# Equal-token attention scores as elementwise products on GpSimd, summed by sixteen small matmuls

## The reference, cut to what matters

```python
q, k, v, a = (c[..., 0], c[..., 1], c[..., 2], c[..., 3])       # complex, per head and channel
mag2 = a.real * a.real + a.imag * a.imag
a = a * (jax.lax.rsqrt(mag2) * jax.nn.sigmoid(jnp.log(mag2)))
kv = jnp.einsum('blhd,blhe->blhde', k, v)
...
_, h = jax.lax.associative_scan(comb, (a_e, kv), axis=1)        # h_t = a_t * h_(t-1) + k_t v_t
y = jnp.einsum('blhd,blhde->blhe', q, h)
```

## Time and profile before

| | |
|---|---|
| device time, 3 runs | 3787.07 us median, 3783.72 to 3789.23 |
| the profiled execution | 3780.13 us, of which its span is 3778.3 us |
| mean granted TensorE clock | 0.828 |
| busy over the span | PE 2900.2 us (77%), DVE 2067.0 (55%), ACT 1153.3 (31%), POOL 652.2 (17%) |
| chain of work that ended last | PE 59%, DVE 19%, ACT 7%, POOL 5%, issue 4% |

### The profile page before, as it was taken

How to read it: one execution, slowest core, us unless ns; L and a number is a source line. 1 busy time by engine, 2 the same in 40 slices (tenths; PEclk the granted TensorE clock), 3 DMA queues, 4 the chain that set the end, 5 groups by cost and what they waited for, 6 DMA issues and landing times.

```text
span 3778.3 us, 81987 instructions
## 1 busy us (share of the span) xinstructions
PE 2900.2 (77%) x35840; PEld 2145.9 (57%) x35840; DVE 2067.0 (55%) x4544; ACT 1153.3 (31%) x2220; POOL 652.2 (17%) x682
## 2 busy tenths in 40 slices
PE   4358869877986898699769877987688549999990
PEld 3244557545744664575457545744554538888880
DVE  4445676576658666856686676658443830000104
ACT  0212353135314432533353135314412512222220
POOL 0322400520060016003400520051000000000006
PEclk8678878888788878798878887888889769999995
DMA  2122201210121122012201220121100016565545
GB/s 81 23 57 51 43 5 42 68 40 15 48 69 19 41 46 56 8 41 57 46 7 41 62 46 8 47 67 24 41 29 28 2 52 205 190 200 192 193 158 174
DMA packets 230022, 247.56 MB, mean 66 GB/s; under 512 B 147360, under 2 KB 187168, under 8 KB 227360
## 3 DMA queue, kind: packets, MB, share of 16 engines
q1 hardware_dynamic: 223520, 225.54, 20.8%
q0 software_dynamic: 6144, 16.79, 1.4%
HBM read 196.15 MB, written 46.14 MB: 64 GB/s over the span
## 4 chain that ended last, share of the span: by engine, by line
PE 59%; DVE 19%; ACT 7%; POOL 5%; issue 4%; DMA 1%; SPq 0%; POOLq 0%; DVEq 0%
PE banks L1816 13%; PE banks L2326 7%; PE banks L2345 7%; PE banks L2049 4%; POOL arena L1708 3%; PE banks L2118 3%; PE banks L2138 2%; PE banks L2143 2%; PE banks L1826 2%; POOL arena L1752 2%; PE banks L2073 2%; PE banks L1948 2%; PE banks L1943 2%; PE banks L1953 1%; PE banks L1922 1%
## 5 line engine op out<-in xcount | busy, mean ns | idle before, releaser
L1708 POOL TENSOR_TENSOR arena<-arena 128x1 f32<-128x1 f32 (+30 forms) x496 | 435.1, 908 | 605.3 <-DMA arena<-n_d 438.2
L1168 DVE TENSOR_REDUCE arena<-arena 128x1 f32<-128x1 f32 (+30 forms) x496 | 243.6, 502 | 173.2 <-POOL arena L1708 168.8
L1729 POOL DMA_INDIRECT h_d<-h_tok,pos_now x64 | 66.4, 1037 | 1570.5 <-DVE pos_now L1573 1553.4
L2118 PE MATMUL banks<-arena 32*32 32x64 f32 (+2 forms) x6144 | 203.2, 317 | 162.3 <-DVE arena L1473 97.1
L1816 PE MATMUL banks<-hT,ring 128*128 128x512 f32 x640 | 310.6, 638 | 9.6 <-DVE arena L1312 8.9
L2118 PE MATMUL banks<-arena,xn 32*32 32x64 f32 (+2 forms) x6144 | 185.5, 305 | 149.1 <-DVE xn L1473 122.1
L2118 PEld LDWEIGHTS banks<-arena 32*32 32x32 f32 (+2 forms) x6144 | 180.3, 191 | 201.7 <-DVE arena L1473 117.1
L2326 PE MATMUL banks<-arena 128*128 128x256 f32 x1248 | 276.8, 381 | 0.0
L2345 PE MATMUL banks<-arena 128*128 128x256 f32 x1248 | 275.7, 380 | 0.0
L1020 ACT ACTIVATE arena<-banks,arena 128x256 f32<-128x256 f32 x312 | 130.7, 470 | 456.1 <-PE banks L2326 456.1
L2118 PEld LDWEIGHTS banks<-arena,xn 32*32 32x32 f32 (+2 forms) x6144 | 171.5, 186 | 167.9 <-DVE xn L1473 135.1
(11 more groups left out here) (340 smaller groups left out, 5251.4 us busy)
## 6 DMA issues: line engine op xcount, KB each, us to landing
arena<-in_w_ring SPq DMA_DIRECT2D x78, 1024.0 KB, 5.1
ring<-in_w_ring SPq DMA_DIRECT2D x104, 512.0 KB, 4.9
arena<-h_d SPq DMA_DIRECT2D x39, 256.0 KB, 5.3
y_d<-arena SPq DMA_DIRECT2D x39, 256.0 KB, 5.8
n_d<-NA SPq DMA_DIRECT2D x8, 1024.0 KB, 3.8
arena<-n_d SPq DMA_DIRECT2D x16, 512.0 KB, 8.1
u_d<-arena SPq DMA_DIRECT2D x8, 1024.0 KB, 3.8
NA<-u_d SPq DMA_DIRECT2D x32, 256.0 KB, 5.8
```

Source lines behind the costliest of these rows:

```text
L1168: dve.tensor_reduce(Usub[:, c, 0:t, t], part, AX.X, ALU.add).then_inc(*up(sub_sum, me))
L1708: pool.tensor_tensor(part, Usub[:, c, 0:t, 0:t], Nsub[:, c, t, 0:t].unsqueeze(1).to_broadcast([P, t, t]), ALU.mult)\
L2118: i_ = mm(bank[4 * hg + h][keys, b * width:(b + 1) * width], K2[rows_, r, b, keys], q, start=(r == 0), stop=(r == 1), skip_group_check=True)
```

## The change

For each hg, GpSimd multiplies q with k of the same token, channel by channel: four products of 128 x 1024 in a segment, two for each hg, written to ring slots 4, 0 and 1 and to `hT`. The two for hg wait for plane 5 (or 11) out of PSUM, for -q, and for `plane_mm` 8 (or 12), the last reader of the slots. PE sums each over the channels of a head with sixteen matmuls of 128 x 128 weights (the products) by 4 columns (`head_of`, ones for a head's channels), where it had 128 matmuls of 32 x 32 weights by 64 columns. DVE spreads the sum with the same predicated copy, whose source is now the sum, broadcast along tokens. The copy now waits for `scored`; the sum into q waits for GpSimd's `same_ok` in its place. On ACT, hg 1's `mag_sqrt` moves ahead of planes 10 and 11, and `take_keys(0)` ahead of `fill_state(1)`. The fills of the ring slots now wait for `scored` of both.

```diff
@@ ScalarE
                                 act.activation(Q3[:, 0], Q3[:, 2], ACT.Copy, scale=-1.0).then_inc(*up(q_neg, me))
-                            if n == 3:
-                                mag_sqrt(0)
-                    mag_sqrt(1)
+                            if c == 3:
+                                mag_sqrt(hg)
...
                     take_outputs(0)
+                    take_keys(0)
                     fill_state(1)
-                    take_keys(0)
                     take_keys(1)
@@ VectorE
                         if k == 0:
+                            dve.wait_ge(*at(scored, hg + 1))
...
-                                banks_[:, 4 * hg:4 * hg + HP, 0:2 * B * BLK].rearrange("p h (g t) -> p h g t", g=2 * B))\
-                                .then_inc(*up(masked, me))
+                                bank[4 * hg][:, 0:HP * 2 * B].rearrange("p (g h) -> p h g", h=HP).unsqueeze(3)
+                                .to_broadcast([P, HP, 2 * B, BLK])).then_inc(*up(masked, me))
...
-                        dve.wait_ge(*at(scored, hg + 1))
+                        dve.wait_ge(*at(same_ok, 2 * (hg + 1)))
                         step(dve.tensor_tensor(q2, t1[:, :, :], t2[:, :, :], ALU.add))
@@ GpSimd
-                    pool.wait_ge(*at(plane_mm, 6 * HG))
+                    for hg in range(HG):
+                        pool.wait_ge(*at(plane_ok, 6 * hg + 6))
+                        pool.wait_ge(*at(q_neg, hg + 1))
+                        pool.wait_ge(*at(plane_mm, 8 + 4 * hg))
+                        for r in range(2):
+                            pool.tensor_tensor(same_token[hg][r].rearrange("p (c t) -> p c t", c=2),
+                                               Q3s[hg][:, 1 - r:3 - r].rearrange("p c b t -> p c (b t)"),
+                                               K2s[hg][:, r].rearrange("p b t -> p (b t)").unsqueeze(1).to_broadcast([P, 2, NT]),
+                                               ALU.mult).then_inc(*up(same_ok, me))
+                    pool.wait_ge(*at(scored, HG))
                     pool.wait_ge(*at(v_mm, B))
@@ TensorE
+                    def same_tokens(hg):
+
+                        pe.wait_ge(*at(same_ok, 2 * (hg + 1)))
+                        if hg:
+                            pe.wait_ge(*at(v3_ok, 1))
+                        for b in range(B):
+                            for c in range(2):
+                                at_ = (2 * b + c) * HP
+                                for r in range(2):
+                                    t = slice(c * NT + b * SEG, c * NT + (b + 1) * SEG)
+                                    i_ = mm(bank[4 * hg][:, at_:at_ + HP], same_token[hg][r][:, t], const("head_of"),
+                                            start=(r == 0), stop=(r == 1))
+                        i_.then_inc(*up(scored))
...
-                    for k in range(STEPS):
+                    pe.wait_ge(*at(plane_ok, 6 * HG))
+                    for b in range(B):
+                        value_columns(b)
+                        if b == 1:
+                            same_tokens(0)
+                    same_tokens(1)
+                    for k in range(1, STEPS):
                         for hg in range(HG):
                             level(hg, k)
```

More of the change, by code:

```diff
@@ L274, in build @@
                  for v in (h_tok[:, :, :].rearrange("p b d -> p (b d)"), y2_flat[:, 2 * NT:4 * NT])]
+        same_token = ((ring[:, 4, :], ring[:, 0, :]), (ring[:, 1, :], hT[:, :, :, :].rearrange("p k b t -> p (k b t)")))
         first_raws = [score[:, :, :, :, SEG - BLK + i * BLK // 2:SEG - BLK + (i + 1) * BLK // 2] for i in range(HG)]
@@ L436, in build @@
         rt_exp = signal("rt_exp", rest=1)
+        same_ok = signal("same_ok", rest=4)
         zeroed = signal("zeroed", rest=6)
@@ L1736, in turn @@
                     settle()
-                counted(seg, [zeroed, sub_mul])
+                counted(seg, [zeroed, sub_mul, same_ok])
                 pool.sem_inc(started.handle, 1)
@@ L2079, in level @@
                         lev = k - 1
-                        if k == 0:
-                            pe.wait_ge(*at(plane_ok, 6 * HG))
+                        if lev:
+                            pe.wait_ge(*at(k_ready, 2 * lev + hg - 1))
+                        if lev == 0:
+                            pe.wait_ge(*at(masked, hg + 1))
                             if hg:
                                 pe.wait_ge(*at(v3_ok, B))
-                        else:
-                            if lev:
-                                pe.wait_ge(*at(k_ready, 2 * lev + hg - 1))
-                            if lev == 0:
-                                pe.wait_ge(*at(masked, hg + 1))
-                            elif lev <= INNER:
-                                pe.wait_ge(*at(block_ok, 2 * (lev - 1) + hg + 1))
-                            else:
-                                pe.wait_ge(*at(laid_middle, hg + 1))
-                        pe.wait_ge(*(at(q_ready, 2 * (k - 1) + hg + 1) if k else at(q_neg, hg + 1)))
+                        elif lev <= INNER:
+                            pe.wait_ge(*at(block_ok, 2 * (lev - 1) + hg + 1))
+                        else:
+                            pe.wait_ge(*at(laid_middle, hg + 1))
+                        pe.wait_ge(*at(q_ready, 2 * lev + hg + 1))
                         for b in range(B):
                             for r in range(2):
-                                for x in range(HP * NCH if k == 0 else 2 * HP if lev == INNER else HP):
+                                for x in range(2 * HP if lev == INNER else HP):
                                     h = x % HP
@@ L2099, in level @@
                                     q = Q3[rows_, 1 - r:3 - r, b]
-                                    if k == 0:
-                                        n = (h + x // HP) % NCH
-                                        keys = slice(BLK * n, BLK * n + BLK)
-                                        q = q[:, :, keys]
-                                        width = 2 * BLK
-                                    elif lev < INNER:
+                                    if lev < INNER:
                                         keys = slice(0, SEG)
@@ L2119, in level @@
                                             start=(r == 0), stop=(r == 1), skip_group_check=True)
-                            if k == 0 and hg == 0:
-                                if b == B - 1:
-                                    i_.then_inc(*up(scored))
-                                value_columns(b)
-                        if k or hg:
-                            i_.then_inc(*up(scored))
+                        i_.then_inc(*up(scored))
                     def outputs(hg):
```

## The result

| | before | after |
|---|---|---|
| median of 7 runs, us | 3783.72 (3771.18 to 3789.23) | 3821.38 (3805.88 to 3829.67) |
| ratio to before, 95% interval | | 1.0096 [1.0083, 1.0109] |
| profiled execution, us | 3780.1 | 3818.91 |
| its span, us | 3778.3 | 3817.1 |
| mean granted clock | 0.828 | 0.808 |

The changed kernel is slower by 1.0%, some 36 us by the ratio and 37.7 us between the medians. It issues 7,104 instructions fewer (74,883 for 81,987), and takes longer.

The account below looks back on a forecast made before the run. No engine bounds the mixer stage; the chain passes between PE, ACT and DVE. Eight segments' +35 us and the keys' -20 gave +15 on 3780.1, so 3795, and 3802 with the runs' 7 us median difference; range 3755 to 3845.

Parts of the forecast that it names:

- step 3: PE's start in the mixer stage, behind plane 11: from 439.2 to 441.3, late by 2.1 us.
- step 4: PE's work until `scored` of hg 1, all at the high clock level: 460.6 against 462.1, a gain of 1.5 us.
- step 5: PE's clock in the mixer stage: falls three times, 3.9 us each, 11.8 us at half speed, costing 5.9 us more.
- step 6: ACT's key copies ahead of the state: outputs(1) 2.95 us earlier in six segments, 1.3 in two, together -20.3 us.
- step 7: The predicated copy's new source, later ring-slot fills and the new wait for `scored` before hg 0's copy: at nothing.
- Step 1: GpSimd's four products of 1024 elements: 2.40 us each.
- Step 2: DVE's L1415 behind GpSimd's products: ends at 439.4 instead of 434.76, 4.6 us later; bounds 0 and 4.8.
- three thin places: On PE, the wait for plane 11 with a one-row bias matmul behind, and two groups of sums; clock falls at each.
- That the clock holds: Rival: PE's clock stays up in the mixer stage, 8 x (-1.5) - 20.3 = -32 us, 3755; chance 0.17.
- That the products don't delay plane 11: Rival: PE starts at 439.2, step 0 changes nothing and the keys' 20 us remain, 3767; chance 0.20.
- Clock low for most of the stage: Rival: PE's clock stays low, `scored` at about 471.5, +9.4 us a segment, +55 in all, 3842; chance 0.15.

Follow-up runs that it names:

- experiment 5: The changed kernel with ACT's root of hg 1 back behind plane 11: 3796.38 us, 0.9956 of the kernel before.
- experiment 6: The changed kernel with GpSimd's first products also waiting until DVE has done the magnitudes: 3795.69 us, 0.9961 of the kernel before.
- experiment 8: The changed kernel with the value columns' bias matmul from 128 equal rows instead of one row: 3763.44 us, 0.9932 of the kernel before.
- Experiment 4: The changed kernel with each group of sums made twice, same results: 3926.95 us, 1.0371 of the kernel before.
- experiment 3: The changed kernel with one more unused 512-column matmul ahead of each batch's sums: 3824.98 us, 1.0109 of the kernel before.
- experiment 9: The changed kernel with GpSimd's products later and the sums in four pieces, one-row bias kept: 3773.67 us, 0.9964 of the kernel before.
- Experiment 1: The kernel before with only take_keys(0) moved ahead of fill_state(1) on ACT: 3765.18 us, 0.9953 of the kernel before; on another chip 3769.97 us, 0.9954.
- experiment 2: The changed kernel with ACT's old order of keys and state: 3835.13 us, 1.0153 of the kernel before.
- Experiment 10: The changed kernel with products later, sums in four pieces and bias from 128 rows: 3769.83 us, 0.9890 of the kernel before; on another chip 3732.40 us, 0.9847.

## Why the prediction was right, and which sizes were off

It was right in its sign and in its mechanisms, and too small in size. As a time, 3802 is 19 us below the measured 3821. As a change, it forecast +15 us and 36 to 38 came, about two and a half times as much; the new time is inside the whole range (3755 to 3845), but 1 us above the forecast's own (3787 to 3820). That it missed by 19 us and not by 22 is luck: the kernel before, 3787 in the three runs that the forecast starts from, was 3783.7 in the seven. Its terms, for all eight segments, beside the measured ones:

| term | forecast, us | measured, us |
|---|---|---|
| step 3, PE starts late | 8 x 2.1 = +17 | 8 x 1.33 = +11 |
| step 4, from PE's start to the copy, all at the high level | 8 x -3.6 = -29 | 8 x -3.9 = -31 |
| step 5, the clock | 8 x 5.9 = +47 | 8 x 7.9 = +63 |
| step 6, the keys | -20 | -20 |
| step 7, behind the copy for hg 1 | 0 | +7.5 |
| elsewhere in the round | 0 | +8 |
| sum | +15 | +39 |

The measured step 4 is worked out from the rows of experiment 5: two value columns and a group of sums at 1.00 take 2.96 + 2.87 + 3.57 us, twice that is 18.8, and before the way from PE's start to the copy took 30.28 - 7.61 = 22.67. The clock is what is left: 35.66 - 8.94 - 18.8 = 7.9.

*Step 1, products of 2.40 us.* 2.35 when alone (2348 ns on average over the eight that follow plane 11's copy). Right.

*Step 2, L1415 late by 4.6.* Late by 3.85. The two engines did exclude each other: each DVE operation ended just behind a product, and experiment 6 gave both operations their old durations back by moving the products alone. They took turns, one DVE operation, one product. It was less than 4.6 because neither operation paid for a product's whole 2.35 us: against experiment 6, L1416 lost 1.93 and L1417 2.03. The rule of the Trainium skill, page "SBUF — State Buffer", section "Who interferes with whom", holds, and the reciprocal beside a product at 3.35 us shows its other half, that a DVE operation with at most one SBUF input, outside the modes that use both ports, does not contend.

*Step 3, PE late by 2.1.* Late by 1.33, on account of step 2. But experiments 5 and 6 price this link at 1.4 points, 53 us, and not at 11: with the longer idle time ahead of the one-row matmul the clock was down at the very start of the stage too (experiment 8, with 128 rows and the same idle time, kept it at 1.00 there). The prediction named that as one of its three thin places, and so had it in step 5, where it belongs.

*Step 4.* Right within 0.3 us per segment, and made up otherwise than it says. It compares PE's end in the new order with the start of DVE's copy in the old one, and calls both `scored`. Before, PE was done at 460.4, and DVE's sum into q and its negation stood between PE's end and the copy, as the chain of work of before shows:

```profile
460.50 1.24 DVE arena L1431
461.76 0.43 DVE arena L1432
```

In the new order the sum into q no longer waits for `scored`, and the copy starts as soon as the sums are done. So some 1.7 of the 3.9 us are DVE's, taken out of the way by the changed wait, and only 2.2 are PE's.

*Step 5, the term that was mis-sized.* The prediction put the low time at three stretches of 3.9 us, 11.8 in all; 7.9 us lost mean 15.8 us at half clock. The 3.9 us were a guess a little above the shortest low stretch in the rows, though it says that some last longer. The trace of before had a longer one than the prediction read: what began at 638 did not end at 645, it went on to 665, with PE busy nearly throughout:

```profile
645.00:665.00 20.00, 18.68 (x202) 16.86 (x195) 11.73 (x34) 12.23 (x20) 4.43 (x5) 0.50 0.07 23
```

The prediction also took the value columns for wide work from end to end. They are wide for two thirds only. The bias, with its one row, is a third of each column's time. Experiment 8 shows what that did: with 128 rows in that one instruction, 6.3 of the 7.9 us are gone (and 1.2 more for the faster columns), while the start is as late as in the changed kernel. Experiment 4 shows the sums' part from the other side: with twice the sums the low stretch is longer and takes in what follows. That the clock is the cause and not the number of matmuls is shown by experiment 3. The one-row matmuls were in the kernel before as well, at 1.00, so by themselves they did not bring the clock down. With the sums beside them they did, a little with PE on time and the sums in two pieces (0.92, experiment 6), more in four pieces (0.79, experiment 9), and most with PE late (0.71 in two pieces, 0.68 in four).

The Trainium skill's rule that TensorE's clock follows how busy it has recently been (page "TensorE: Matmul & The Clock Gate", section "What's actually happening") doesn't hold here if busy is read as busy time: 18.00 us of 18.00 busy at 0.50, against 17.22 of 18 at 1.00.

*Step 6, the keys.* -19.6 us for -20.3, 2.9 us in six segments and 1.1 in two. Experiment 1 measured it alone at 0.47%, 18 us.

*Step 7.* The predicated copy was not held up by GpSimd's fill of the ring slots, which the prediction had left open: 1.31 us beside the MEMSET at 469.20, 1.29 at 451.19 with none beside it. What was not at nothing is the 0.93 us per segment between the copy and outputs(0). On that way stand groups of 64 small matmuls that take 2.1 or 3.8 us by the clock they meet, and which of them meet the low level differs between the traces; experiments 6 and 10 have it too (77.1 and 76.9 us for 75.4). That is read from the traces and wasn't tested.

*The +8 us elsewhere* lie between outputs(1) and the next segment's plane 7. The trace of experiment 1, in which only the keys' order differs, has about 9 us more there than that of before as well, so they don't belong to the scores. The traces point to the keys' order: the seven stretches take 1610.4 us before and 1610.0 in experiment 2, which have the old order, and 1619.2 in experiment 1 and 1619.9 in the changed kernel, which have the new one. But experiment 3, with the new order, has 1612.7, so how much is chance between executions stays open.

*The rivals.* That the clock holds was wrong: the rows show 0.50. Experiment 10, in which it holds, with PE on time besides, was at 0.9890 and 0.9847; the rival's 3755 is 0.9916. That the products don't delay plane 11 was wrong here, but experiments 5 and 6 brought about its case, and it came out at -0.4%, where the rival had 3767, -0.5%. "Clock low for most of the stage" (+55 us) is nearer to what happened in three of the eight segments, which had 0.59 to 0.60, than the forecast is; the mean lies between the two.

## What to carry to other kernels

When a change replaces matmuls by fewer and smaller ones, don't stop at their sum: look at the granted clock of the stage before and after, and list the thin work around them, one-row bias matmuls too. One cheap edit on the work that stays (here the bias from 128 rows, 1.2 to 1.6 points) can be worth more than the work removed. Before moving elementwise work to an idle GpSimd, look at which two-input DVE operations run at that moment and who waits for them; here one more wait on GpSimd's side took the delay away and cost nothing that the time shows (0.9961, as with the root late).

## What the hardware showed that I had not expected

- The rows of the bias matmul changed the granted clock of the stage. The bias matmul has records of the same length with 1 row (1.12 us for two) as with 128 (1.13), but with 128 rows a value column took 0.3 us less from start to start, the stage's granted clock was 0.92 instead of 0.71, and the kernel was 1.6 points faster (0.9932 for 1.0096, on different chips; 1.2 points, 0.9847 for 0.9964, on the same one).
- Work could be added for almost nothing. Eight wide matmuls more per segment, 61 us at the high level, cost some 5 us, with the stage's clock at 0.92 instead of 0.71.
- With operations queued on both sides, DVE (two SBUF inputs) and GpSimd took turns operation by operation: L1416 3.16 us for 1.23, L1417 2.72 for 0.69, and a product 3.21 us (the mean of the sixteen that follow plane 7) for 2.35 alone. A predicated copy that reads PSUM was not held up by a GpSimd MEMSET (1.31 us for 1.29). But one SBUF input alone is no promise: in seven of the eight segments, before and after alike, DVE's 1 + m of hg 0 (a TENSOR_SCALAR of 512 elements that reads and writes SBUF) took 3.2 to 3.6 us beside GpSimd's fill of 4096 elements, and ended 0.28 us behind it each time; with nothing beside it, it takes 0.43.
- Small matmuls with 128 x 128 weights and 4 columns go at 0.11 us each at the high level (3.57 us for 32, start to start) and 0.21 at the low one (462.31 to 469.07 in the changed kernel's first segment, 32 of them).
